# A routed expert layer: gate weights applied before the rows are stored, and gathers that add into the residual

## The chip, the cores and the metric

The kernel runs on one core of a Trainium2 chip. The time is that of the device for one launch, in microseconds (us). The core has a matrix engine (PE, its weight loads shown apart as PEld), a vector engine (DVE), an activation engine (ACT), a general engine (GpSimd, shown as POOL) and SyncE (SP), which here only starts transfers. DVE and ACT read PSUM, where PE writes; transfers and GpSimd reach only the on-chip memory (SBUF) and DRAM.

## What is computed

A decoder of two layers on x of shape 8 x 512 x 256, in float32, each layer with an attention, a cross attention and a feed-forward part, every part added to the residual stream. The change touches the first layer's feed-forward part, a mixture of 32 experts of which each token takes 4, and the part right after it, a linear recurrence. Cut to what matters:

```python
def L0_ffn(x):                                # xf: 4096 tokens x 256
    scores = softmax(xf @ Wg)                 # 32 gates for each token
    weights, indices = top_k(scores, 4)
    for e in range(32):
        pos = nonzero(pair_expert == e, size=C, fill_value=P)
        out = (silu(xg @ W1[e]) * (xg @ W3[e])) @ W2[e] * w[:, None]
        y = y.at[tok].add(out)
    return y + swiglu(xf, Ws1, Ws2, Ws3)      # and a shared expert
x = x + L0_ffn(layernorm(x))
def L1_attn(u):                               # h = h * A + u_t over the 512 positions
    return hs @ BC
x = x + L1_attn(layernorm(x))
```

## The kernel before

x stays in SBUF as `x[P, NT, D]`: 32 tiles of 128 tokens by 256 numbers, four tiles (`TB`) to a batch, eight batches (`B`). Each engine runs a program of its own, in the order in which it is written, and waits on semaphores. Stages end with a barrier. Three stages follow one another in `mix_experts_routed` and `mix_recurrence`.

**Ahead of them** the gates of all tokens are computed (`gates`, `[P, 32 tiles, 32 experts]`), and for each token and each of its four choices the row in which it shall stand (`place`): the rows of DRAM tensor `places` are sorted by expert, each expert filled up to whole tiles of 128, 160 tiles in all (`TILES`). `places` was cleared during the first attention by 23 transfers on SP (L2441).

**The scatter stage** (L1651 to L1777). For each batch and tile DVE writes the normalized rows `xn` and the indices `now` (L1738, L1740). GpSimd waits for them and issues four indirect transfers (L1694, `TOP` = 4), which scatter the tile's 128 rows of 1 KB to `places`. Buffer j is written again when its four scatters have landed (`scattered[j]`). DVE then works out from `rank`, `top` and `gates` the four weights of each token (`weight`, L1744 to L1750) and serves the shared expert, which PE and ACT compute. After batch 0 it also builds the table that says which expert each of the 160 tiles has (L1766 to L1771; `expert_h` and `expert_y`, the same table at two offsets).

**The expert stage** (L1782 to L1917). 160 tiles, in loops of `UNROLL` = 8. SP loads a tile of `places` to `xt` (L1805, eight buffers) as soon as PE has transposed the tile that stood there (`xp_full`), and stores the result `y` to DRAM tensor `outputs` (L1809) four tiles later. PE transposes, multiplies by `w1`, transposes, multiplies by `w2`, each a tile or more behind the other, and loads the expert numbers of eight tiles to registers at each turn. DVE forms `hid` (L1905) and copies the product out of PSUM to `y` (L1911).

**The gather stage** (`mix_recurrence`). For each batch, tile and choice GpSimd issues an indirect transfer (L639) that gathers 128 rows of `outputs` into a buffer `row`. DVE waits for a pair of tiles, adds weight times row into x (L698, eight multiply-adds for a pair, those of one tile in turn), gives GpSimd the next indices (`now`, L703), and goes on with the recurrence: of this batch the statistics and `xn`, of the batch before the scan (L735), of the one before that the addition of the result (L728). PE transposes and multiplies, ACT takes a square root.

An adding scatter stands already in the last stage of the kernel, the second layer's experts: L2287 adds 128 rows (`oa`) and 32 rows (`ob`) for each of 64 experts into `out` in DRAM, and L2277 gathers as many rows (`xa`, `xb`, 1280 bytes each).

## Time and profile before

| | us |
|---|---|
| median of 3 runs | 2944.31 |
| lowest, highest | 2944.04, 2954.93 |
| the profiled execution | 2948.37 |
| its span in the trace | 2946.6 |
| PE busy | 2320.9 (79%) |
| DVE busy | 1308.5 (44%) |
| ACT busy | 825.8 (28%) |
| GpSimd busy | 813.1 (28%) |

The profile is that of one execution. The span goes from the first to the last recorded instruction. A share of the whole span says little here, since the kernel is a row of stages with different limits, so the stages have to be looked at one by one. A row of a timeline has the start and the length in us, then engine, line, operation, the tile written and the tiles read; what stands in brackets is how long the engine had been idle and what ended that. Of an indirect transfer, the length is what GpSimd spends on issuing it; the data lands later, and "to landing" is counted from the start of the issue.

### The profile page before, as it was taken

The numbers are of one execution on the slowest core, as the hardware profiler recorded it, in microseconds if no ns is written. First come the engines' busy times: TensorE is split into PE (matmuls) and PEld (weight loads), VectorE is DVE, ScalarE is ACT, GpSimd is POOL, SyncE is SP. The second block draws the span as 40 slices with busy tenths as digits, with TensorE's granted clock in tenths as the row PEclk, the third lists the DMA queues.
The fourth block names the chain that finished last, engine by engine and source line by source line (L and its number), as shares of the span: only waits on it lengthen the run. The fifth ranks groups of instructions, "written<-read, shape, count | busy, mean of one in ns | idle before, by whom it ended". The sixth has DMA issues, their size and how long they took to land. (4 is left out here: it accounts for less than half of the span.)

```text
span 2946.6 us, 41569 instructions
## 1 busy us (share of the span) xinstructions
PE 2320.9 (79%) x12030; PEld 1614.8 (55%) x12031; DVE 1308.5 (44%) x2759; ACT 825.8 (28%) x1860; POOL 813.1 (28%) x1110
## 2 busy tenths in 40 slices
PE   5888656355799913348888888589988999999998
PEld 2444643133677712223333333245548999999997
DVE  4344225543233337747676665474442222222222
ACT  1111211111344410026666666122211222121221
POOL 1000000167100057412112120022224544455543
PEclk9999766677899966669999999789999999999999
DMA  8200110252444423232222220220005777777775
GB/s 268 94 0 0 47 40 1 84 204 102 138 146 146 143 87 100 62 101 91 84 84 82 82 67 1 81 100 15 14 21 182 239 254 237 245 251 237 253 242 168
DMA packets 191238, 353.01 MB, mean 120 GB/s; under 512 B 29302, under 2 KB 165983, under 8 KB 182984
## 3 DMA queue, kind: packets, MB, share of 16 engines
q1 hardware_dynamic: 160456, 294.68, 29.2%
q0 software_dynamic: 30720, 57.60, 8.1%
q8 instruction: 27, 0.44, 0.1%
q14 instruction: 35, 0.29, 0.0%
HBM read 259.21 MB, written 92.40 MB: 119 GB/s over the span
## 5 line engine op out<-in xcount | busy, mean ns | idle before, releaser
L2342 PE MATMUL me_hp<-me_xgT,me_w 128*128 128x160 f32 x3072 | 440.4, 300 | 0.8 <-DVE me_xgT L2384 0.6
L2342 PEld LDWEIGHTS me_hp<-me_xgT,me_w 128*128 128x128 f32 x3072 | 424.6, 191 | 1.9 <-DVE me_xgT L2384 0.7
L1335 DVE TENSOR_REDUCE hd_nmax<-hd_wide 128x2 f32<-128x1024 f32 x256 | 306.5, 1220 | 151.2 <-PE hd_wide L1127 151.1
L1286 ACT ACTIVATE hd_prob<-hd_slim 128x512 f32<-128x512 f32 x512 | 275.8, 601 | 158.7 <-PE hd_slim L1138 158.0
L2398 DVE TENSOR_TENSOR me_hid<-me_act_out,me_hp 128x160 f32<-128x160 f32 x384 | 123.2, 321 | 372.1 <-ACT me_act_out L2370 372.1
L2351 PE MATMUL me_op<-me_hid,me_w 128*128 128x160 f32 x1536 | 235.9, 303 | 0.0
L1127 PE MATMUL hd_wide<-hd_k_stack,hd_q_stack 97*128 97x512 bf16 x512 | 198.8, 393 | 34.9 <-DVE hd_rest L1330 15.0
L639 POOL DMA_INDIRECT rc_row<-outputs,rc_now x128 | 129.5, 1011 | 345.4 <-DVE rc_now L685 306.4
L2370 ACT ACTIVATE me_act_out<-me_hp 128x160 f32<-128x160 f32 x384 | 116.4, 303 | 358.1 <-PE me_hp L2342 358.1
L2351 PEld LDWEIGHTS me_op<-me_hid,me_w 128*128 128x128 f32 x1536 | 213.7, 190 | 2.6
L1138 PE MATMUL hd_slim<-hd_q_stack,hd_k_stack 100*128 100x512 bf16 x512 | 195.1, 384 | 16.5 <-DMA hd_q_stack<-hd_nrows 11.1
L2055 PE MATMUL me_r_hp<-me_r_xnT,me_r_sw 128*128 (+1 forms) x384 | 168.9, 600 | 10.9 <-DMA me_r_sw<-in_L_ffn_shared_w2T 10.9
L1852 PE MATMUL mr_e_hp<-mr_w,mr_e_xtT 128*128 x640 | 167.3, 384 | 0.8 <-issue 0.6
L1150 PE MATMUL hd_pv<-hd_prob,hd_v 128*32 128x512 f32 x1024 | 136.4, 604 | 6.6 <-ACT hd_oT L1252 6.2
L1138 PEld LDWEIGHTS hd_slim<-hd_q_stack,hd_k_stack 100*128 100x128 bf16 x512 | 49.5, 98 | 167.2 <-ACT hd_prob L1286 71.2
L1694 POOL DMA_INDIRECT places<-mr_s_xn,mr_s_now x128 | 125.8, 983 | 52.4 <-issue 36.0
L652 PE MATMUL rc_outp<-rc_wbc,rc_hid 128*128 128x256 f32 x128 | 46.8, 544 | 108.8 <-DVE rc_hid L735 108.8
L1905 DVE TENSOR_TENSOR mr_e_hid<-mr_e_act_out,mr_e_hp 128x128 f32<-128x128 f32 x160 | 46.1, 288 | 192.3 <-ACT mr_e_act_out L1884 192.3
L2055 PEld LDWEIGHTS me_r_hp<-me_r_xnT,me_r_sw 128*128 128x128 f32 x384 | 73.9, 193 | 101.1 <-issue 89.7
L2044 POOL TENSOR_TENSOR me_r_hid<-me_r_act_out,me_r_up_out 128x512 f32<-128x512 f32 x48 | 65.2, 1358 | 214.8 <-ACT me_r_up_out L2092 214.8
L2287 POOL DMA_INDIRECT out_x<-me_oa,me_then_a x64 | 104.4, 1631 | 68.7 <-issue 62.2
L1852 PEld LDWEIGHTS mr_e_hp<-mr_w,mr_e_xtT 128*128 128x128 f32 x640 | 110.1, 192 | 10.4 <-issue 1.6
(393 smaller groups left out, 3693.6 us busy)
## 6 DMA issues: line engine op xcount, KB each, us to landing
me_w<-in_L_ffn_w_exp SPq DMA_DIRECT2D x64, 2304.0 KB, 9.1
places<-z_zero SPq DMA_DIRECT2D x23, 896.0 KB, 10.1
mr_e_xt<-places SPq DMA_DIRECT2D x160, 128.0 KB, 2.0
outputs<-mr_e_y SPq DMA_DIRECT2D x160, 128.0 KB, 1.9
part_rows<-hd_parts SPq DMA_DIRECT2D x48, 256.0 KB, 2.3
hd_k_stack<-part_rows SPq DMA_DIRECT2D x192, 64.0 KB, 2.2
hd_q_stack<-part_rows SPq DMA_DIRECT2D x192, 64.0 KB, 2.2
mr_w<-in_L_ffn_w_in SPq DMA_DIRECT2D x4, 2048.0 KB, 18.2
```

Source lines behind the costliest of these rows:

```text
L639: nc.gpsimd.indirect_dma_start(out=row[:, j, n, :], out_offset=None, in_=outputs[:, :], in_offset=bass.IndirectOffsetOnAxis(ap=now[:, j, n ...
L1127: last = nc.tensor.matmul(wide[:, at, j, :], q_stack[0:FIRST_ROWS, bt.slot, h, qc * P:(qc + 1) * P], k_stack[0:FIRST_ROWS, bt.slot, h, :], ...
L1138: nc.tensor.matmul(slim[:, slim_slot(bt, item), :], k_stack[:, bt.slot, h, kc * P:(kc + 1) * P], q_stack[:, bt.slot, h, :], start=True, st ...
L1150: last = nc.tensor.matmul(pv[32 * j:32 * j + 32, :], v[:, slot, kc, head(g, j), :], prob[:, kc * GH + j, :], start=(kc == 0), stop=(kc == ...
L1286: nc.scalar.activation(prob[:, u, :], slim[:, slim_slot(bt, item), :], ACT.Exp, scale=D ** -0.5)\
L1335: nc.vector.tensor_reduce(nmax[:, g % 2, n // 2, c:c + 2], wide[:, at], AX.X, ALU.max, negate=True)\
L1694: nc.gpsimd.indirect_dma_start(out=places[:, :], out_offset=bass.IndirectOffsetOnAxis(ap=now[:, j, n:n + 1], axis=0), in_=xn[:, j, :], in_ ...
L1852: last = nc.tensor.matmul(hp[:, v, 0:2 * F], xtT[:, v, c, :], w1[:, bass.ds(e, 1), c, :].rearrange("p a n -> p (a n)"), start=(c == 0), st ...
L2055: last = nc.tensor.matmul(hp[:, f % 2, half, :], sw1[:, c, at:at + P], xnT[:, c, bass.ds(b * S, S)], start=(c == 0), stop=(c == DC - 1))
L2342: last = nc.tensor.matmul(hp[:, f % 3, half * CAP:(half + 1) * CAP], w1[:, sl, c, cols], xgT[:, sl, c, :], start=(c == 0), stop=(c == DC - 1))
L2351: last = nc.tensor.matmul(op[:, c, 0:CAP], w2[:, sl, f, c * P:(c + 1) * P], hid[:, sl, f, :], start=(f == 0), stop=(f == FC - 1))
L2398: nc.vector.tensor_tensor(hid[:, sl, f, :], act_out[:, f % 2, :], hp[:, f % 3, 0:CAP], ALU.mult).then_inc(h_free, 1)
```

## The change

Each scattered row carries the 32 gates of its token behind its 256 numbers, so rows of `places`, `xn` and `xt` have 288 numbers and the scattered ones come with a small copy on DVE. In the expert stage the copy of the product out of PSUM becomes a multiplication by one column of `xt`, the gate of the tile's expert, whose number DVE reads from a register; DVE loads eight such registers at each turn of the loop. Since `xt` is now read until then, SP loads a slot only behind the store of the tile that stood there. The match that gave `weight` goes. In the gather stage the buffer `row` and the multiply-adds go: each gather adds into x by itself (`compute_op=ALU.add`). Two additions into a tile may not overlap, so GpSimd waits before each for the one before it in the same tile, and takes the four tiles in turn for each choice. Its loop over the batches is written out.

```diff
@@ mix_recurrence, GpSimd
-                with pool.Fori(0, B) as b:
-                    for j in range(TB):
-                        pool.wait_ge(now_ready, b * TB + j + 1)
-                        pool.sem_inc(passed, 1)
-                        for n in range(TOP):
-                            nc.gpsimd.indirect_dma_start(out=row[:, j, n, :], out_offset=None, in_=outputs[:, :],
-                                                         in_offset=bass.IndirectOffsetOnAxis(ap=now[:, j, n:n + 1], axis=0))\
-                                .then_inc(gathered[j], 16)
+                for b in range(B):
+                    for n in range(TOP):
+                        for j in range(TB):
+                            if n == 0:
+                                pool.wait_ge(now_ready, b * TB + j + 1)
+                            else:
+                                pool.wait_ge(gathered[j], (b * TOP + n) * 16)
+                            pool.sem_inc(passed, 1)
+                            nc.gpsimd.indirect_dma_start(out=x[:, b * TB + j, :], out_offset=None,
+                                                         in_=outputs[:, :],
+                                                         in_offset=bass.IndirectOffsetOnAxis(ap=now[:, j, n:n + 1], axis=0),
+                                                         compute_op=ALU.add).then_inc(gathered[j], 16)
@@ mix_recurrence, DVE
-                    for pair in range(0, TB, 2):
-                        for j in range(pair, pair + 2):
-                            dve.wait_ge(gathered[j], b * 16 * TOP + 16 * TOP)
-                        for m in range(2 * TOP):
...
-                            nc.vector.scalar_tensor_tensor(xs, row[:, j, n, :], weight[:, bass.ds(t, 1), n], xs, ALU.mult, ALU.add)\
-                                .then_inc(taken, 1)
-                        dve.wait_ge(taken, (b * TB + pair + 2) * TOP)
+                    for j in range(TB):
+                        dve.wait_ge(gathered[j], (b + 1) * 16 * TOP)
                         if more:
-                            for j in range(pair, pair + 2):
-                                nc.vector.tensor_copy(now[:, j, :], place[:, b * TB + j + TB, :]).then_inc(now_ready, 1)
+                            nc.vector.tensor_copy(now[:, j, :], place[:, b * TB + j + TB, :]).then_inc(now_ready, 1)
@@ mix_experts_routed, the scatter stage
-                            nc.vector.tensor_scalar(xn[:, j, :], x[:, t, :], mean[:, bass.ds(t, 1)], rstd[:, bass.ds(t, 1)],
+                            nc.vector.tensor_scalar(xn[:, j, 0:D], x[:, t, :], mean[:, bass.ds(t, 1)], rstd[:, bass.ds(t, 1)],
                                                     ALU.subtract, ALU.mult).then_inc(rows_ready, 1)
+                            nc.vector.tensor_copy(xn[:, j, D:D + E], gates[:, t, :]).then_inc(rows_ready, 1)
                             nc.vector.tensor_copy(now[:, j, :], place[:, t, :]).then_inc(rows_ready, 1)
...
-                        nc.vector.tensor_tensor(match[:], rank[:, ts, :].unsqueeze(2).to_broadcast(wide),
-                                                top[:, ts, 0:TOP].unsqueeze(3).to_broadcast(wide), ALU.is_equal).then_inc(matched, 1)
-                        dve.wait_ge(matched, b * 2 + 1)
-                        nc.vector.tensor_tensor(match[:], match[:], gates[:, ts, :].unsqueeze(2).to_broadcast(wide), ALU.mult)\
-                            .then_inc(matched, 1)
-                        dve.wait_ge(matched, b * 2 + 2)
-                        nc.vector.tensor_reduce(weight[:, ts, :], match[:], AX.X, ALU.add).then_inc(weighed, 1)
@@ mix_experts_routed, the expert stage
-                            if not last:
-                                sp.wait_ge(xp_full, n + 1)
-                                load(n + UNROLL, u)
                             if not (first and u < LAG_S):
                                 store(n - LAG_S, (u - LAG_S) % UNROLL)
+                                if not (last and u >= LAG_S):
+                                    load(n - LAG_S + UNROLL, (u - LAG_S) % UNROLL)
...
+                        dve.load(regs_y, expert_y[0:1, bass.ds(i * UNROLL, UNROLL)])
...
-                                nc.vector.tensor_copy(y[:, v, :], yp[:, v % 2, 0:D]).then_inc(y_ready, 1)
+                                e = dve.snap(regs_y[u], min_val=0, max_val=E - 1)
+                                nc.vector.tensor_scalar(y[:, v, :], yp[:, v % 2, 0:D], xt[:, v, bass.ds(e + D, 1)], None, ALU.mult)\
+                                    .then_inc(y_ready, 1)
@@ program
-        ("places", [161 * P, D], F32), ("outputs", [161 * P, D], F32),
+        ("places", [161 * P, D + 32], F32), ("outputs", [161 * P, D], F32),
-            zero = Kit(nc, early, "z_").sb("zero", [P, ROWS, D])
+            zero = Kit(nc, early, "z_").sb("zero", [P, ROWS, D + 32])
```

GpSimd, the gather stage, before: the head of the loop and its first tile. `rc_now` holds the indices, `rc_row` the gathered rows.

```order
L634 UNCONDITIONAL_BRANCH
L634 ISA
L639 DMA rc_row<-outputs,rc_now 128x256 [waits rc_now_ready]
L639 DMA rc_row<-outputs,rc_now 128x256 x3
L636 REGISTER_ALU
```

GpSimd, the same place in the changed kernel: batch 0 as far as its second addition into each tile. `all_x` is the residual stream.

```order
L641 DMA all_x<-outputs,rc_now 128x256 [waits rc_now_ready] x4
L641 DMA all_x<-outputs,rc_now 128x256 [waits all_gathered0]
L641 DMA all_x<-outputs,rc_now 128x256 [waits all_gathered1]
L641 DMA all_x<-outputs,rc_now 128x256 [waits all_gathered2]
L641 DMA all_x<-outputs,rc_now 128x256 [waits all_gathered3]
```

Four gathers of one tile in a row have become one of each of the four tiles, and from the second round on each waits for the landing of the one before it in its tile.

DVE in the expert stage, before: the first tile of its loop.

```order
L1914 ISA
L1905 TENSOR_TENSOR mr_e_hid<-mr_e_act_out,mr_e_hp 128x128 [waits mr_silu_done]
L1908 REGISTER_ALU
L1910 REGISTER_ALU [waits mr_yp_full]
L1911 COPY mr_e_y<-mr_e_yp 128x256 [waits mr_y_stored5]
L1904 REGISTER_ALU
```

DVE, the same place in the changed kernel.

```order
L1900 ISA
L1883 TENSOR_LOAD mr_expert_y
L1889 TENSOR_TENSOR mr_e_hid<-mr_e_act_out,mr_e_hp 128x128 [waits mr_silu_done]
L1892 REGISTER_ALU
L1894 REGISTER_ALU [waits mr_yp_full]
L1895 ISA [waits mr_y_stored5]
L1896 TENSOR_SCALAR mr_e_y<-mr_e_yp,mr_e_xt 128x256
```

A load of registers stands at the loop's head, ahead of the first `hid`, and the copy has become a multiplication by a column of `xt` with one instruction more ahead of it.

SP in the expert stage, before: one tile of its loop.

```order
L1805 ISA [waits mr_xp_full]
L1805 DMA mr_e_xt<-places 128x256
L1808 REGISTER_ALU
L1809 ISA [waits mr_y_ready]
L1809 DMA outputs<-mr_e_y 128x256
```

SP, the same place in the changed kernel: the wait for PE's transpose is gone, and the load stands behind the store.

```order
L1791 ISA [waits mr_y_ready]
L1791 DMA outputs<-mr_e_y 128x256
L1787 ISA
L1787 DMA mr_e_xt<-places 128x288
L1790 REGISTER_ALU
```

The store has moved ahead, and the load is issued after `y` of the tile four before is done.

## Rows read from the trace of the kernel before

**Rows 1.** Stretches: length, busy of PE, PEld, DVE, ACT, POOL, clock, DMA share, GB/s.
```profile
570.00:753.00 183.00, 102.74 (x256) 60.06 (x256) 63.49 (x131) 19.82 (x24) 126.05 (x129) 0.75 0.46 165
753.00:1049.00 296.00, 268.79 (x1440) 220.24 (x1440) 107.58 (x320) 132.56 (x480) 0.00 (x0) 0.98 0.45 142
1049.00:1253.00 204.00, 55.03 (x192) 43.89 (x192) 131.14 (x355) 11.91 (x16) 129.46 (x128) 0.63 0.29 84
```

**Rows 2.** Timeline of the gather stage: start, length, engine, operation, [idle before <-releaser].
```profile
1055.25 1.01 POOL L639 DMA_INDIRECT rc_row<-outputs,rc_now  x1 [306.42 <-DVE rc_now L685]
...
1222.76 0.95 POOL L639 DMA_INDIRECT rc_row<-outputs,rc_now  x1 [0.30 <-issue]
1225.61 3.26 DVE L698 SCALAR_TENSOR_TENSOR all_x<-rc_row,rt_weight,all_x 128x256 f32<-128x256 f32 x8 [5.24 <-DMA rc_row<-outputs,rc_now]
1228.90 1.28 DVE L728 TENSOR_TENSOR all_x<-all_x,rc_outp 128x512 f32<-128x512 f32 x2
...
1251.26 1.41 DVE L731 BATCH_NORM_STATS2 all_stats<-all_x 128x6 f32<-128x256 f32 x4
```

**Rows 3.** Tile `rc_row`: min/median/max in ns, first and last start, landing.
```profile
L639 POOL DMA_INDIRECT rc_row<-outputs,rc_now x128: 949/953/2066, 1055.2 to 1222.8; - x128
...
DMA to landing us min/median/max: 2.7/2.7/3.8
```

**Rows 4.** Line 1694, the scatters: the same columns.
```profile
L1694 POOL DMA_INDIRECT places<-mr_s_xn,mr_s_now x128: 965/969/1810, 572.1 to 747.9; - x128
```

**Rows 5.** Timeline of the scatter stage, batch 1 and the last scatter.
```profile
604.78 0.15 DVE L1740 COPY mr_s_now<-rt_place 128x4 int32<-128x4 int32 x1
...
605.74 1.81 POOL L1694 DMA_INDIRECT places<-mr_s_xn,mr_s_now  x1 [12.57 <-DVE mr_s_now L1740]
...
606.74 0.69 DVE L1747 TENSOR_TENSOR mr_s_match<-mr_s_match,mr_gates 128x512 f32<-128x512 f32 x1
...
747.87 0.96 POOL L1694 DMA_INDIRECT places<-mr_s_xn,mr_s_now  x1 [0.30 <-issue]
```

**Rows 6.** Timeline of the expert stage, around a turn of its loop.
```profile
768.49 0.42 DVE L1911 COPY mr_e_y<-mr_e_yp 128x256 f32<-128x256 f32 x1
769.26 0.43 PE L1846 MATMUL mr_e_xp<-all_ident,mr_e_xt 128*128 128x128 f32 x2 [0.81 <-issue]
...
770.96 0.29 DVE L1905 TENSOR_TENSOR mr_e_hid<-mr_e_act_out,mr_e_hp 128x128 f32<-128x128 f32 x1 [2.05 <-ACT mr_e_act_out L1884]
...
783.57 0.43 PE L1846 MATMUL mr_e_xp<-all_ident,mr_e_xt 128*128 128x128 f32 x2 [1.01 <-issue]
```

**Rows 7.** GpSimd in the last stage, by form: count | busy us, mean ns | idle before.
```profile
L2287 POOL DMA_INDIRECT out_x<-me_oa,me_then_a x62 | 101.2, 1632 | 66.9 <-issue 62.2 <-POOL me_then_b L2269 4.7
L2287 POOL DMA_INDIRECT out_x<-me_ob,me_then_b x61 | 82.9, 1360 | 18.6 <-issue 18.6
L2277 POOL DMA_INDIRECT me_xa<-token_rows,me_now_a x59 | 62.0, 1051 | 53.2 <-POOL me_now_b L2269 51.0 <-issue 2.2
L2277 POOL DMA_INDIRECT me_xb<-token_rows,me_now_b x59 | 52.3, 887 | 18.0 <-issue 18.0
```

**Rows 8.** DMA queue of GpSimd: packets, MB, share; 1055 to 1223, 2236 to 2940 us.
```profile
q0 software_dynamic: 6048, 16.52, 34.0%
...
q0 software_dynamic: 16944, 22.67, 17.9%
```

**Rows 9.** GpSimd from 2217 to 2230 us, by form, ahead of the first scatter.
```profile
L2277 POOL DMA_INDIRECT me_xa<-token_rows,me_now_a x3 | 2.9, 981 | 2.5 <-POOL me_now_b L2269 2.5
```

**Rows 10.** Tile `me_oa`: ns min/median/max, and the landing of its scatters.
```profile
L2390 DVE TENSOR_SCALAR me_oa<-me_tp,me_xa x64: 476/477/486, 2235.8 to 2935.1; 128x256 f32<-128x256 f32 x64
...
DMA to landing us min/median/max: 3.8/4.5/4.6
```

**Rows 11.** The page, DMA issues: count, KB each, us to landing.
```profile
places<-z_zero SPq DMA_DIRECT2D x23, 896.0 KB, 10.1
mr_e_xt<-places SPq DMA_DIRECT2D x160, 128.0 KB, 2.0
```

More of the change, by code:

```diff
@@ L581, in mix_correlation, with mix_recurrence @@
         s.clear()
-def mix_recurrence(nc, ctx, x, ident, stats, mean, rstd, outputs, gathered, place, weight, decay_in, w_bc):
+def mix_recurrence(nc, ctx, x, ident, stats, mean, rstd, outputs, gathered, place, decay_in, w_bc):
     with ExitStack() as own:
@@ L592, in mix_recurrence @@
         TOP = place.shape[2]
-        row = k.sb("row", [P, TB, TOP, D])
         now = k.sb("now", [P, TB, TOP], I32)
@@ L1511, in softmax_scores, with mix_experts_routed @@
     chain.link(nc.vector.tensor_tensor(logits[:], logits[:], total[:].unsqueeze(2).to_broadcast([P, NT, n]), ALU.mult))
-def mix_experts_routed(nc, ctx, x, ident, mean, rstd, w_gate, w_in, w_out, places, outputs, scattered, place, weight):
+def mix_experts_routed(nc, ctx, x, ident, mean, rstd, w_gate, w_in, w_out, places, outputs, scattered, place):
     with ExitStack() as own:
@@ L1655, in mix_experts_routed @@
             k2 = Kit(nc, own2, "mr_s_")
-            xn = k2.sb("xn", [P, TB, D])
+            xn = k2.sb("xn", [P, TB, D + E])
             now = k2.sb("now", [P, TB, TOP], I32)
@@ L1671, in mix_experts_routed @@
             y_full, y_free = s.sem("sh_y_full"), s.sem("sh_y_free")
-            numbered, tabled, matched, weighed = s.sem("numbered"), s.sem("tabled"), s.sem("matched"), s.sem("weighed")
+            numbered, tabled = s.sem("numbered"), s.sem("tabled")
             with nc.Block() as block:
@@ L1690, in _ @@
                         for j in range(TB):
-                            pool.wait_ge(rows_ready, (b * TB + j) * 2 + 2)
+                            pool.wait_ge(rows_ready, (b * TB + j) * 3 + 3)
                             pool.sem_inc(passed, 1)
@@ L1754, in batch @@
                         dve.wait_ge(y_full, b + 1)
-                        dve.wait_ge(rows_ready, b * 2 * TB + 2 * TB)
+                        dve.wait_ge(rows_ready, b * 3 * TB + 3 * TB)
                         for m in range(2):
@@ L1783, in mix_experts_routed @@
             k2 = Kit(nc, own2, "mr_e_")
-            xt = k2.sb("xt", [P, UNROLL, D])
+            xt = k2.sb("xt", [P, UNROLL, D + E])
             xtT = k2.sb("xtT", [P, 2, DC, P])
@@ L1897, in _ @@
                     dve.sem_inc(y_ready, 2)
+                    regs_y = [dve.alloc_register(f"weigh_y{u}") for u in range(UNROLL)]
                     def steps(i, first, last_ones):
+                        dve.load(regs_y, expert_y[0:1, bass.ds(i * UNROLL, UNROLL)])
                         for u in range(UNROLL):
@@ L2442, in clear_rows @@
                         .then_inc(cleared, 16)
-                sp.dma_start(outputs[(n_tiles - 1) * P:n_tiles * P, :], zero[:, 0, :]).then_inc(cleared, 16)
+                sp.dma_start(outputs[(n_tiles - 1) * P:n_tiles * P, :], zero[:, 0, 0:D]).then_inc(cleared, 16)
             with nc.Block() as block:
@@ L2469, in program @@
             place = r.sb("place", [P, NT, TOP], I32)
-            weight = r.sb("weight", [P, NT, TOP])
             mix_experts_routed(nc, ctx, x, ident, mean, rstd, a["L0_ffn_Wg"], a["L0_ffn_w_in"], a["L0_ffn_w_out"], places, outputs,
-                               scattered, place, weight)
-            mix_recurrence(nc, ctx, x, ident, stats, mean, rstd, outputs, gathered, place, weight, a["L1_attn_A"], a["L1_attn_BC"])
+                               scattered, place)
+            mix_recurrence(nc, ctx, x, ident, stats, mean, rstd, outputs, gathered, place, a["L1_attn_A"], a["L1_attn_BC"])
         norm_stats(nc, ctx, "l1x", x, stats, mean, rstd, fresh=True)
```

11 lines of the change are left out of this document (1 added, 10 removed).

## The prediction

> **What bounds the kernel now.** I read first the table of busy times by stage [rows 1]. The change touches three stages that follow one another: the scatter stage (570 to 753 us), the expert stage (753 to 1049) and the gather stage, which also holds the recurrence (1049 to 1253). The reader is to see that PE, the busiest engine of the whole, is idle for most of the first and the last: 102.74 of 183 us and 55.03 of 204 us. It is busy 268.79 of 296 us in the middle one.
>
> Next I read the gather stage in order of time [rows 2]. GpSimd issues the first gather at 1055.25 and the last, the 128th, at 1222.76, which is 127 steps of 1.319 us. A gather occupies GpSimd for 0.953 us by the median [rows 3], and 0.30 us pass before the next. An undisturbed step is thus 1.258 us, 127 of them are 159.8 us, and the remaining 7.7 us are gathers that took longer. DVE stands waiting for the last pair of tiles: its multiply-add starts at 1225.61, 2.85 us after the last gather's issue. From 1228.90, when it ends, a serial tail of the last batches runs to 1252.67, and then the next stage begins. So this stage lasts as long as 128 issues on GpSimd, plus a landing, plus a tail. DVE's arithmetic between them is beside the path, but for the last eight multiply-adds (3.29 us).
>
> The scatter stage is bound by the same engine in the same way: a scatter takes 0.969 us by the median [rows 4], and from 605.74 to 747.87 there are 111 steps of 1.280 us [rows 5].
>
> The expert stage goes by PE. DVE, SP and their transfers have room: where PE turns around its loop it waits 0.81 us for nothing but its own registers and branch, and DVE then idles 2.05 us; eight tiles take 14.31 us [rows 6].
>
> **The gather stage, part by part.** Removed from DVE are 128 multiply-adds. All but the last eight lie beside GpSimd's issues, so their going gives nothing by itself. The last eight give 3.29 us. With them goes most of what stretched the gathers: the 7.7 us above. The scatter stage, in which DVE does less, has (1.280 - 1.273) x 111 = 0.8 us of such stretch, so I leave 1 us and book a gain of 6.7.
>
> Added is the addition inside each gather. No row shows a gather that adds. The nearest rows are the scatters of the last stage that add into `out` [rows 7]: 1.632 us for 128 rows and 1.360 us for 32 rows, against 1.051 and 0.887 us for that stage's plain gathers of as many rows. Adding costs GpSimd 0.58 us at 128 rows and still 0.47 us at 32. Direction is no explanation: the plain scatter and the plain gather of 128 rows differ by 0.016 us (0.969 and 0.953) [rows 3, 4]. The packets say that an adding DMA is built differently. The 126 or so plain gathers of the gather stage make 6048 packets, 48 each, for 128 rows. The last stage has some 62 experts with a plain gather of 128 rows (48) and of 32 rows (32), and 16944 packets, 273 for an expert; 193 are left for the two adding scatters with 160 rows together, so a row has a packet of its own [rows 8]. I take this as a price of the addition and not of its target.
>
> The last stage makes GpSimd a little slower than here: its own 128-row gathers take 0.981 us while no scatter is yet in it [rows 9] and 1.051 us later. The adding gather then lies between 0.953 + 0.58 = 1.53 us and 1.63 us. I take 1.55, near the lower end, since the plain gather of this stage is the one that it replaces. With the 0.30 us gap a step is 1.855 us, and 127 steps are 235.6 us where 159.8 stood: 75.8 us more. The ends of the price that I keep for the range are 1.36 us, what 32 adding rows take (127 x 0.19 = 24 us less), and 1.66 us plus a gap of 0.31 (15 us more).
>
> Added too is a wait for each gather: the next addition into a tile is not issued before the one before it has landed. Behind it on GpSimd are all the later gathers, and DVE waits for these. A tile's turn comes every fourth step, 7.4 us after its last issue. Plain gathers land after 2.7 us, at most 3.8 [rows 3]; adding scatters of 128 rows land after 4.5 us, at most 4.6, in a stage whose queues are fuller [rows 10]. So the wait is over 2.8 us before it is asked: nothing. At the batch's turn DVE copies `now` once a tile's last gather has landed, some 4.6 us after issue, and DVE has been waiting by then: it is busy 131 us in the whole stage before, multiply-adds among it, which is 16.4 us for a batch, and the new batch takes 16 x 1.855 = 29.7 us. Nothing again.
>
> The tail: the last landing comes about 4.0 us after its issue where it was 2.85, and the 3.29 us of multiply-adds are gone: -2.1.
>
> Gather stage: +75.8 - 6.7 - 2.1 = **+67.0 us**.
>
> **The scatter stage.** Rows become 1152 bytes instead of 1024. The 128-row gather of 1280 bytes takes 0.981 us [rows 9] against 0.953 for 1024; a quarter to a half of 0.028 us on 112 scatters is 1 us. The number of scatters stays. DVE loses three wide operations in a batch (0.69 us each) and gets four small copies (0.15 us each, as the `now` copies) [rows 5]. Before the first scatter of batch 1, for which GpSimd waits 12.57 us, DVE builds the table, and ahead of that it waits for PE; the operations lost in batch 0 lie before that wait and give nothing, and the scatter comes one small copy later: 0.2. From there DVE is ready before GpSimd, with more room than before. **+1 us**, bounds 0 and +4.
>
> **The expert stage.** The copy out of PSUM, 0.42 us, becomes a multiplication by a column of `xt`; the same form stands in the last stage with 0.477 us [rows 10]. 0.05 us more moves nobody where DVE's two operations, 0.42 and 0.29 us, share the 1.79 us of a tile. New is a load of eight registers on DVE at each turn of the loop. PE loads sixteen there and loses 0.81 us; DVE is free from 768.91 to 770.96, 2.05 us [rows 6]. Cover: 1.2 us. If it were gone, 20 turns would pay. On SP the load of a slot now stands behind the store, hence behind `y_ready`: it is issued about four tiles ahead (7 us) instead of seven and lands after 2.0 us [rows 11], so 5 us of cover stay. Behind it on SP is only the next store. **0 us.**
>
> **The clearing of `places`** gets an eighth more bytes (23 transfers of 896 KB [rows 11] become 1008 KB) on a queue that nobody waits for in the attention stage. 0 us, at most 1.
>
> **Sum:** +67.0 + 1 = **+68 us**. The profiled run took 2948.37 us (span 2946.6 and 1.8 around it), 4.1 above the median of the three. It would become 3016; from the median, 2944.3 + 68 = **3012 us**.
>
> **Rivals.** *A: the addition is done by the DMA engines and costs GpSimd nothing* (the side of no loss). Against it are both adding kinds of [rows 7]; for it, only that these write to DRAM and these gathers write to SBUF. Place: every step of the gather stage; price of 0.58 us gone. The stage then gives 6.7 + 2.1 back and the sum is -9 + 1 = -8: 2936 us. It comes out at no loss as soon as the adding gather costs less than about 0.07 us above the plain one, since 127 x 0.07 is the 9 us of gain. The Trainium skill, "DMA: Bandwidth & Descriptors", section "SWDGE vs HWDGE vs iDMA", says that GpSimd computes one pair of descriptors for each DMA operation, a read and a write, and names no extra for one that adds. By that rule this rival would be right; the trace disagrees for scatters, 1.632 against 1.051 us. Chance 0.10.
>
> *B: half price.* An addition into SBUF needs less preparation than one into DRAM: about 1.25 us each, 127 x 0.3 = 38 us less than forecast, 2974 us. No row speaks for it but the missing case. 0.07.
>
> *C: the landing takes over.* If a 128-row adding gather took longer than 7.4 us to land, GpSimd would wait for each. At 9 us a step is 2.25 us and the time is 3012 + 50 = 3062 us. Against it: 4.6 us at most [rows 10]. For it: one packet a row, and a read of two sources. 0.06.
>
> *D: DVE's register load is long*, 3 us rather than under 1. Then each of 20 turns loses about 1 us: 3032 us. Against it is PE's 0.81 us for twice as many registers. 0.05.
>
> **How the numbers follow.** The forecast has 0.72: its own range is 2986 (1.36 us each) to 3030. With B at the lower and D at the upper side the range of 8 in 10 is 2980 to 3042; outside lie A, B and C. A measurement of this kernel tells apart about 0.5%, 15 us. Faster by more than that needs under 2930 us, which no case gives: 0.03 for what I have not seen. Within 0.5%: A, 0.11. Slower: 0.86.
>
> **What would show it.** In the profile after: adding gathers on GpSimd of 1.5 to 1.65 us, 0.30 us apart, with no waits for a landing; the gather stage about 65 us longer; PE's turn in the expert stage unchanged at 14.3 us for eight tiles; scatters at 0.97 to 0.98 us. I am wrong if the adding gather takes about 0.95 us (A), if GpSimd's idle time names the DMA (C), or if PE's wait at the loop's turn grows (D).

## The result and the profile after

| | before | after |
|---|---|---|
| median, us | 2946.94 | 3014.63 |
| lowest, highest, us | 2944.04, 2954.93 | 3005.80, 3027.62 |
| the profiled execution, us | 2948.37 | 3006.31 |
| its span, us | 2946.6 | 3004.5 |

The changed kernel is slower: the ratio of the times is 1.0229, with a 95% interval of 1.0177 to 1.0280. The medians lie 67.7 us apart. On a second chip the same pair gave 3019.64 against 2957.00 us, a ratio of 1.0220 (1.0179 to 1.0261).

The first view is the one that the prediction began with, the table of busy times by stretch, now of the kernel after: length, busy time of PE, PEld, DVE, ACT and GpSimd (with the number of instructions), granted clock of PE, DMA share, GB/s. The three rows answer to those of [rows 1].

```profile
570.00:754.70 184.70, 105.20 (x256) 61.53 (x256) 53.25 (x140) 19.82 (x24) 124.67 (x129) 0.74 0.48 175
754.70:1050.00 295.30, 269.89 (x1440) 221.23 (x1440) 123.60 (x320) 132.74 (x480) 0.00 (x0) 0.98 0.50 151
1050.00:1321.50 271.50, 55.06 (x192) 43.80 (x192) 79.13 (x227) 11.91 (x16) 198.89 (x128) 0.60 0.45 63
```

Only the last row has grown by much. DVE has lost 52 us of work there and GpSimd has got 69.43 us more (198.89 against 129.46) for the same 128 instructions; the stretch itself is longer by about as much. The adding gathers themselves, by their source line, in the kernel after (name, count, ns min/median/max, first and last start, then the idle time before them by what ended it, then who waited):

```profile
L641 POOL DMA_INDIRECT all_x<-outputs,rc_now x128: 1542/1552/1665, 1056.3 to 1292.4; - x128
its engine sat idle before it (us, times) until:
  DVE rc_now L688: 305.7, 1
  issue: 36.9, 121
  DMA all_x<-outputs,rc_now: 1.8, 6
...
  DVE rc_now L695: 153.3, 28
...
DMA to landing us min/median/max: 3.7/3.8/3.9
```

Where [rows 3] had 953 ns for one gather and 2.7 us to its landing, there are now 1552 ns and 3.8 us. The largest is 1665 ns: nothing stretches them any more. Six gaps name a landing, with 1.8 us together, which is 0.30 us each and thus the gap that every gather has; GpSimd has waited for no landing. DVE, on the other hand, waits 153 us for gathers. In order of time the end of the stage reads so (columns as in [rows 2]):

```profile
1292.37 1.55 POOL L641 DMA_INDIRECT all_x<-outputs,rc_now  x1 [0.30 <-issue]
1296.38 1.29 DVE L720 TENSOR_TENSOR all_x<-all_x,rc_outp 128x512 f32<-128x512 f32 x2 [20.30 <-DMA all_x<-outputs,rc_now]
...
1319.27 1.41 DVE L723 BATCH_NORM_STATS2 all_stats<-all_x 128x6 f32<-128x256 f32 x4
```

From the issue of the last gather to the first addition of the recurrence's result there are 4.01 us; before there were 6.14 (1222.76 to 1228.90 in [rows 2]), 2.85 for the landing and 3.29 for eight multiply-adds.

To compare stages across kernels I cut each profiled run at the same five events: the first scatter, the last scatter, the first gather, the last gather, and the start of the next stage. All are in us.

| | before | after | after minus before | predicted |
|---|---|---|---|---|
| first scatter to last | 175.8 | 177.2 | +1.4 | +1 |
| last scatter to first gather | 307.4 | 306.7 | -0.7 | 0 |
| first gather to last | 167.5 | 236.0 | +68.5 | +69.1 |
| last gather to next stage | 34.7 | 33.6 | -1.1 | -2.1 |
| sum | 685.4 | 753.5 | +68.1 | +68 |

The two spans differ by 57.9 us only, and that is no contradiction. The way to the first scatter takes 572.1 and 572.4 us, but the part behind the three stages takes 1689.1 us before and 1678.5 after, with no instruction changed in it. 8.8 of these 10.6 us lie in one stretch of the second layer; here it is by the same columns as above, first in the kernel before, then in the one after:

```profile
1855.60:1978.60 123.00, 92.39 (x280) 49.08 (x281) 67.82 (x169) 24.80 (x32) 18.81 (x11) 0.82 0.25 85
```

```profile
1923.30:2037.50 114.20, 84.67 (x280) 45.82 (x281) 69.27 (x169) 24.80 (x32) 16.75 (x11) 0.89 0.27 91
```

The same 280 matmuls keep PE busy for 92.39 and 84.67 us, and the granted clock is 0.82 and 0.89. Such stretches differ from one run to the next, whatever the kernel: up to the first scatter, where all kernels of this study are alike but for the size of the clearing, the profiled runs took from 570.7 to 585.8 us. That is why the runs below are compared by the events first, and by the total only where enough runs stand behind it.

### The profile page after: what moved, and what is told of

It reads as the page before. It is cut to its first block and busy times, and to the rows that moved or that the text cites. A ratio compares the mean times of both kernels' runs of the same rounds, so it can differ in the third digit from the quotient of the medians.

```text
span 3004.5 us, 41474 instructions
## 1 busy us (share of the span) xinstructions
PE 2316.3 (77%) x12030; PEld 1614.0 (54%) x12031; DVE 1263.7 (42%) x2640; ACT 825.8 (27%) x1860; POOL 879.7 (29%) x1110
## 3 DMA queue, kind: packets, MB, share of 16 engines
q0 software_dynamic: 43008, 59.70, 10.1%
## 5 line engine op out<-in xcount | busy, mean ns | idle before, releaser
L641 POOL DMA_INDIRECT all_x<-outputs,rc_now x128 | 198.9, 1554 | 344.4 <-DVE rc_now L688 305.7
L2337 PE MATMUL me_op<-me_hid,me_w 128*128 128x160 f32 x1536 | 236.0, 304 | 0.0
L1119 PE MATMUL hd_wide<-hd_k_stack,hd_q_stack 97*128 97x512 bf16 x512 | 198.5, 393 | 35.1 <-DVE hd_rest L1322 15.0
L1685 POOL DMA_INDIRECT places<-mr_s_xn,mr_s_now x128 | 124.4, 972 | 55.3 <-issue 32.9
L655 PEld LDWEIGHTS rc_outp<-rc_wbc,rc_hid 128*128 128x128 f32 x128 | 35.8, 287 | 179.6 <-DVE rc_hid L727 171.7
```

Of the source, the lines that this page charges most:

```text
L641: nc.gpsimd.indirect_dma_start(out=x[:, b * TB + j, :], out_offset=None, in_=outputs[:, :], in_offset=bass.IndirectOffsetOnAxis(ap=now[:, ...
L1119: last = nc.tensor.matmul(wide[:, at, j, :], q_stack[0:FIRST_ROWS, bt.slot, h, qc * P:(qc + 1) * P], k_stack[0:FIRST_ROWS, bt.slot, h, :], ...
L1685: nc.gpsimd.indirect_dma_start(out=places[:, :], out_offset=bass.IndirectOffsetOnAxis(ap=now[:, j, n:n + 1], axis=0), in_=xn[:, j, :], in_ ...
L2337: last = nc.tensor.matmul(op[:, c, 0:CAP], w2[:, sl, f, c * P:(c + 1) * P], hid[:, sl, f, :], start=(f == 0), stop=(f == FC - 1))
```

## The experiments

My theory was that of the prediction: the whole loss is the price that GpSimd pays for issuing an indirect transfer that adds, and this price belongs to the instruction more than to its rows. The rivals were that the loss comes from elsewhere in the change (the wider rows, DVE's new operation in the expert stage, the order of the gathers, the written-out loop), that the wait for the landing costs part of it, and that the price goes by rows. The first four kernels ran on one chip, where the kernel before took 2959.44 us (2951.81 to 2967.71); the other three on another, where it took 2957.00 (2944.45 to 2964.27). The stretches between the events, in us, of all runs:

| | scatters | to first gather | gathers | behind | sum |
|---|---|---|---|---|---|
| before | 175.8 | 307.4 | 167.5 | 34.7 | 685.4 |
| after | 177.2 | 306.7 | 236.0 | 33.6 | 753.5 |
| after once more | 177.7 | 306.2 | 236.0 | 33.3 | 753.2 |
| plain gathers into x | 177.3 | 306.2 | 161.4 | 32.8 | 677.6 |
| DVE adds | 174.5 | 306.0 | 162.3 | 35.1 | 677.9 |
| DVE adds, once more | 176.6 | 306.6 | 163.8 | 34.6 | 681.6 |
| tile by tile | 178.2 | 306.6 | 500.0 | 32.4 | 1017.1 |
| 32 rows added | 177.3 | 306.7 | 211.1 | 33.2 | 728.3 |
| DVE adds, table early | 164.5 | 306.0 | 162.4 | 34.9 | 667.8 |

### The same kernel without the addition

```diff
-                                                         in_offset=bass.IndirectOffsetOnAxis(ap=now[:, j, n:n + 1], axis=0),
-                                                         compute_op=ALU.add).then_inc(gathered[j], 16)
+                                                         in_offset=bass.IndirectOffsetOnAxis(ap=now[:, j, n:n + 1], axis=0)).then_inc(gathered[j], 16)
```

The gathers overwrite the tile of x instead of adding to it, so the addition of the routed results is left out. All else of the change stands, its order and its waits too.

> The changed kernel, but its 128 gathers write plainly over the tiles of x instead of adding into them; waits, order and everything else stay. The addition, and with it the routed result and the residual up to there, is left out. Theory (the addition itself is what costs GpSimd): a gather takes 0.95 to 0.98 us instead of 1.552, the step is 1.26 us, the gather stage is 127 x 0.60 = 76 us shorter and the kernel takes 2930 to 2942 us, below the kernel before. Rival (the wait on each landing, the order or the written-out loop cost part of it): the step stays above 1.35 us or GpSimd's idle time names the DMA, and the time is 2950 us or more.

Measured: 2944.46 us (2934.62 to 2950.61), 0.9935 of the kernel before (0.9911 to 0.9959). The gathers by their line:

```profile
L641 POOL DMA_INDIRECT all_x<-outputs,rc_now x128: 949/953/1107, 1069.3 to 1230.6; - x128
...
  DVE rc_now L694: 2.0, 2
...
DMA to landing us min/median/max: 2.7/2.7/3.1
```

One argument of the instruction was taken away, and with it went 599 ns of each gather, 1.1 us of each landing, and 74.7 us of the time between first and last gather (236.03 to 161.36), where 127 x 0.599 is 76.1. The other 1.4 us are two gaps in which GpSimd now waits for indices from DVE, 2.0 us together where two plain gaps take 0.6. The rest of the change, left alone, is not slower than the kernel before. The forecast in microseconds looks missed by a little (2944 against at most 2942) only because the kernel before stood at 2959 on this chip; as a difference it is -15, where the events show -7.8 (677.6 against 685.4), the remainder being within what untouched stretches vary.

### The weighting alone: plain gathers, DVE adds

```diff
-                for b in range(B):
-                    for n in range(TOP):
-                        for j in range(TB):
...
-                            nc.gpsimd.indirect_dma_start(out=x[:, b * TB + j, :], out_offset=None,
...
+                            nc.gpsimd.indirect_dma_start(out=row[:, j, n, :], out_offset=None, in_=outputs[:, :],
...
-                        dve.wait_ge(gathered[j], (b + 1) * 16 * TOP)
+                            dve.wait_ge(gathered[j], b * 16 * TOP + 16 * TOP)
...
+                            nc.vector.tensor_tensor(xs, row[:, j, n, :], xs, ALU.add).then_inc(taken, 1)
```

The first half of the change stays (gates in the rows, weighting out of PSUM), the second is undone: the gather stage is that of the kernel before, with an addition where the multiply-add stood.

> The weighting part of the change alone: gates travel with the rows and are applied as the product leaves PSUM, but the gathers write plainly to the row buffer as before and DVE adds the rows (128 plain additions of two tiles). Theory: the weighting part costs nothing on the path, so the time is that of the kernel before within 3 us, 2942 to 2950 us; the gather stage is as long as before (204 us). The stretch of the gathers (7.7 us before, 0.5 us with the adding gathers) comes back if DVE's operations on two tiles in SBUF cause it. Rival: the loads behind the stores, the register loads or the wider rows cost something, 5 to 15 us more than before, in the expert or the scatter stage.

Measured: 2946.41 us (2933.93 to 2956.00) against 2959.44, 0.9953 (0.9930 to 0.9976). On the second chip the same kernel was run again, for a closer verdict:

> The kernel of e2_dve_adds once more, so that the next one can be held against it: weights applied in the expert stage, plain gathers, DVE's plain additions. Theory (it shortens the stretch of the gathers and the scatter stage by 7 to 8 us together): 0.994 to 0.998 of the kernel before. Rival (the 13 us of e2_dve_adds were a drift of the chip): a ratio whose interval holds 1.

Measured: 2950.33 us (2931.89 to 2955.57) against 2957.00, 0.9977 (0.9952 to 1.0001). The weighting half therefore costs nothing that can be measured and may bring a quarter to half a per cent. Both expectations come out only in part. The first had the time within 3 us of the kernel before, and it is 13 us below it on that chip, clear of 1 by its interval. The second named an interval that holds 1 as the sign that those 13 us were the chip's drift, and the interval does hold 1, by a hair; so a gain in the total is not shown. By the events the sum is 677.9 and 681.6 against 685.4 us. Where the few microseconds come from is in the gathers (first of the two runs):

```profile
L639 POOL DMA_INDIRECT rc_row<-outputs,rc_now x128: 949/953/1154, 1060.9 to 1223.2; - x128
```

Undisturbed, 127 steps would be 159.8 us. With the multiply-adds DVE had stretched them by 7.7 us, in the one profile that there is of that kernel; with plain additions, which read two tiles of SBUF just as well, it is 2.5 and 4.0 us, and 2.6 in the last kernel below. Of the 4.0 us, 1.7 belong to a single gather, which took 2.702 us:

```profile
L639 POOL DMA_INDIRECT rc_row<-outputs,rc_now x128: 947/953/2702, 1068.0 to 1231.8; - x128
```

This I had not thought: half of the stretch or more goes with the multiplication alone, without taking DVE out of the stage. Eight additions take 2.77 us in that trace where eight multiply-adds take 3.26 [rows 2], so they are a little shorter, but by 15% only; whether it is the form of the operation or its place beside the issues that counts, no run here tells apart.

### Four additions to one tile in a row

```diff
-                    for n in range(TOP):
-                        for j in range(TB):
+                    for j in range(TB):
+                        for n in range(TOP):
```

Only the order of the adding gathers is changed; now three of four wait for the landing of the one just before.

> The changed kernel with the two inner loops of GpSimd swapped: the four additions into one tile follow one another, each after the landing of the one before. Theory: the wait, free in the changed kernel since a tile's turn comes every 7.4 us, is now paid: three steps in four take the landing time, 3.8 us and a little more, 32 x (3 x 4.0 + 1.86) = 443 us where 236 stood, and the kernel takes about 3220 us. Rival (what is waited for is done when the issue ends, and only the issue counts): 3005 to 3030 us as the changed kernel.

Measured: 3284.65 us, one run. By the gathers' line, then in order of time:

```profile
L641 POOL DMA_INDIRECT all_x<-outputs,rc_now x128: 1541/1550/1631, 1069.3 to 1569.3; - x128
...
  DMA all_x<-outputs,rc_now: 289.2, 95
...
DMA to landing us min/median/max: 3.6/3.8/3.9
```

```profile
1073.99 1.56 POOL L641 DMA_INDIRECT all_x<-outputs,rc_now  x1 [3.08 <-DMA all_x<-outputs,rc_now]
1078.57 1.54 POOL L641 DMA_INDIRECT all_x<-outputs,rc_now  x1 [3.02 <-DMA all_x<-outputs,rc_now]
```

Here the wait that the changed kernel has is laid open. A waited step takes 4.58 us (1073.99 to 1078.57): 3.8 to the landing, and 0.8 more before the next gather's row begins. I had taken the landing alone, 4.0, and so expected 443 us for the stage; 96 waited steps of 4.6 and 31 others of 1.85 make 499, and 500.0 were measured. That is most of what the forecast of 3220 us for the kernel fell short by. For the changed kernel this says how near the wait is: a tile's turn comes after four steps, 7.4 us, and 4.6 are needed. With two tiles in turn (3.7 us) it would wait; that was not run.

### Only 32 of 128 rows added

```diff
-                            nc.gpsimd.indirect_dma_start(out=x[:, b * TB + j, :], out_offset=None,
+                            nc.gpsimd.indirect_dma_start(out=x[0:32, b * TB + j, :], out_offset=None,
...
-                                                         in_offset=bass.IndirectOffsetOnAxis(ap=now[:, j, n:n + 1], axis=0),
+                                                         in_offset=bass.IndirectOffsetOnAxis(ap=now[0:32, j, n:n + 1], axis=0),
```

The other 96 rows of each tile are left without their routed results.

> The changed kernel, but each adding gather takes the first 32 of its 128 rows only; the other 96 rows of each tile stay without their routed result. Theory (the addition has a price for each instruction, 0.45 us or more, beside one for each row): an adding gather of 32 rows takes 1.27 to 1.36 us, the kernel 2978 to 2992 us. Rival (the price goes by rows alone, 0.60 us for 128 of them): 1.02 us, and the kernel takes about 2947 us.

Measured: 2997.42 us, one run. That is 38 us above the kernel before on this chip (2959.44); the forecast of 2978 to 2992 us, made from a kernel before of 2947, meant 31 to 45 us more.

```profile
L641 POOL DMA_INDIRECT all_x<-outputs,rc_now x128: 1343/1348/1502, 1068.6 to 1279.7; - x128
```

With a quarter of the rows a gather still takes 1.348 us. From 32 to 128 rows it grows by 0.204 us, 2.1 ns for a row. Carried on straight to no rows at all that leaves 1.28 us, an estimate from two points. The rival by which the price goes by rows wanted about 1.02 us and falls. The last stage had said the same of scatters, 1.360 us for 32 rows and 1.632 for 128 [rows 7], and its price for 32 rows is nearly the one measured here. A plain gather of 32 rows was not run in this stage. Since a plain one of 128 rows takes 0.953 us, and the last stage has the plain one cheaper at 32 rows than at 128, the addition costs 0.40 us or more at 32 rows; by the last stage it is 0.47 there and 0.58 at 128 rows. Splitting these gathers would not bring the time down: four of 32 rows need 4 x 1.65 us with their gaps, one of 128 needs 1.86.

### The changed kernel once more

> The changed kernel unaltered, beside the kernel before and the two below on one chip. Theory (the change costs 68 us between the first scatter and the stage behind the gathers, and the rest of its difference is PE's clock in stages that it does not touch): that stretch is again 753 to 754 us long against 685 before, while the time as a whole may scatter by some 10 us to either side of 68 us above the kernel before. Rival (the 58 us between the two profiled runs is the true price and something in the change gives 10 us back in later stages): the later stages are again 10 us shorter than those of the kernel before.

Measured: 3019.64 us (3017.05 to 3024.21) against 2957.00, that is 62.6 us more. The gathers take 236.0 us again, and the sum of the events is 753.2 where the first run had 753.5. The rival wanted the stages behind to be 10 us shorter again. They take 1685.3 us, where the first profile of this kernel had 1678.5 and that of the kernel before 1689.1; the other kernels, unchanged there, have 1681.3 to 1688.4. So those 10 us are no part of the change. Against the kernel with the weighting alone (681.6, same chip) the second half of the change costs 71.6 us, and against the medians of the same chip 69.3.

### The weighting alone, with the table built earlier

The profile before had shown GpSimd idle for 12.57 us in the scatter stage, until DVE wrote the rows of batch 1 [rows 5], since DVE first served the shared expert of batch 0 and built the expert table. This kernel starts from the one with plain gathers. DVE builds the table right behind the rows of batch 0 and writes the rows of the next batch ahead of the addition of this one's shared expert.

```diff
-                    def batch(b, sl, first):
+                    def rows(b, first):
...
+                    def batch(b, sl, more=True):
...
+                        if more:
+                            rows(b + 1, False)
...
-                    batch(0, 0, True)
+                    rows(0, True)
...
-                    batch(1, 1, False)
+                    batch(0, 0)
+                    batch(1, 1)
```

> The kernel of e6_dve_adds_again with one more edit in the scatter stage: DVE builds the table of experts right behind the rows of batch 0, and writes the rows of batch b + 1 ahead of the addition of batch b's shared result. Theory (GpSimd is the bound of this stage and stands idle 11 to 15 us for the first rows of batch 1): that idle time falls under 3 us, the scatter stage and the kernel get 10 to 14 us shorter than e6_dve_adds_again, about 0.990 of the kernel before. Rival (what is late next is the shared expert's chain through PE, which then ends the stage): GpSimd waits for DVE in later batches or the stage ends by PE, and nothing is gained.

Measured: 2931.46 us (2925.07 to 2939.66), 0.9926 of the kernel before (0.9904 to 0.9948): faster than either kernel of this case, by 25.5 us and by 88. The scatters by their line, first in the repeated run without this edit, then with it:

```profile
L1692 POOL DMA_INDIRECT places<-mr_s_xn,mr_s_now x128: 965/969/1342, 584.8 to 761.4; - x128
...
  DVE mr_s_xn L1736: 14.8, 1
```

```profile
L1692 POOL DMA_INDIRECT places<-mr_s_xn,mr_s_now x128: 965/969/1717, 570.7 to 735.3; - x128
its engine sat idle before it (us, times) until:
  issue: 32.9, 108
  DVE mr_s_now L1739: 7.0, 19
```

The one long idle time is gone, and the scatters take 164.5 us instead of 176.6. Of the 18.9 us between the two medians of this chip, 12.1 are this, within the 10 to 14 that were forecast; the rest lies in stretches that the edit does not touch, the gathers among them (1.4 us). The experiment confirms how the prediction read the scatter stage: what GpSimd waits for counts whole there. What DVE computes beside it is not free altogether: the scatters that now run beside the table's construction take longer (the last section shows them), and GpSimd's 128 scatters together take 126.8 us where they took 124.4. 14.8 us of idle time less these 2.4 are about the 12 that were won.

## Why the prediction was right

**What bounds the stage.** GpSimd's issues in a row. The run without the addition changed their length alone, and the stage followed by 74.7 of 76.1 us; the other 1.4 are a wait for indices that shorter gathers lay open.

**The price of an adding gather**, 1.55 us, was the term on which all hung, and no row showed such a gather. It measured 1.552. Two choices made it: to read the adding scatters of another stage as the price of the addition and not of the scatter or of its target, and to stay near the lower end, because the plain gathers of that stage are slower than here. 127 x (1.552 - 0.953) is 76.1 us where 75.8 had been summed. That it came so close is in part luck: the rows gave 1.53 to 1.63 us, which is 13 us over 127 steps, and nothing in them told 1.55 from the rest. The lower bound that I kept, 1.36 us, is what 32 rows cost, and has turned out to be just that, 1.348, and not a possible price for 128.

**The stretch** of the plain gathers was booked as 6.7 us of gain and 1 us left. With the gap at 0.305 us (36.9 us in 121 gaps), as it is in the 1.258 and 1.855 of the prediction, 127 undisturbed steps of 1.857 are 235.8 us, and 236.0 were measured: 0.2 us are left, so the gain was 7.5. The mechanism is right. What it belongs to is told more exactly by the experiments: a kernel that keeps DVE's additions and drops the multiplication gets 3.7 to 5.2 of these microseconds as well.

**The landing and the wait.** Forecast as about 4.0 us, measured 3.8 by the line and 4.01 at the end of the stage; the wait was free as said. The margin was put at 2.8 us (7.4 less 4.6 for the slowest landing of another stage). It is 2.8 us by chance, since it has other parts: 3.8 to land and, as the run tile by tile shows, 0.8 until GpSimd goes on.

**The tail** was to be 2.1 us shorter. It is, as far as the addition of the recurrence's result (6.14 to 4.01 us), but the whole way to the next stage is shorter by 1.1 only. Half of the other microsecond lies between that addition and the last statistics (22.36 us before, from 1228.90 to 1251.26; 22.89 after, from 1296.38 to 1319.27), and half between these and the next stage's first instruction (6.24 and 6.72 us). What lengthened them is open.

**The scatter stage** got +1.4 us for +1, and scatters of 1152 bytes take 0.969 us as those of 1024 did, by the median. So the wider row, for which the microsecond was booked, costs nothing, and that the number came out is luck. The idle time before batch 1, which I had put at 0.2 more, has grown from 12.57 to 15.34 us, and GpSimd's scatters together take 1.4 us less (124.67 us busy against 126.05 in [rows 1]); the two make 1.4. In the kernel before, then in the one after:

```profile
575.43 8.84 PE L1710 MATMUL mr_s_hp<-mr_xnT,mr_s_sw 128*128 x16 [18.97 <-DMA mr_s_sw<-in_L_ffn_w_out]
590.71 1.61 DVE L1766 TENSOR_TENSOR mr_s_past<-mr_s_tile_no,mr_ends 1x1408 f32<-1x1408 f32 x1
591.42 1.75 POOL L1694 DMA_INDIRECT places<-mr_s_xn,mr_s_now  x1 [0.30 <-issue]
```

```profile
576.62 10.05 PE L1701 MATMUL mr_s_hp<-mr_xnT,mr_s_sw 128*128 x16 [19.91 <-DMA mr_s_sw<-in_L_ffn_w_out]
593.12 1.61 DVE L1749 TENSOR_TENSOR mr_s_past<-mr_s_tile_no,mr_ends 1x1408 f32<-1x1408 f32 x1
608.24 1.01 POOL L1685 DMA_INDIRECT places<-mr_s_xn,mr_s_now  x1 [15.34 <-DVE mr_s_xn L1729]
```

PE's product for the shared expert of batch 0, for whose weights it waits, began later and took longer (8.84 and 10.05 us). So DVE began the table 20.7 us after the first scatter instead of 18.6, and 2.1 of the 2.8 us are this. The rest is that the last scatter of batch 0 took 1.75 us beside the table's first comparison in the kernel before, while in the one after it took 0.97 and was over before the table began, so GpSimd's idle time starts sooner. This is no cost of the change that could be told from chance: the two runs of the kernel with DVE's additions, alike to the letter but run on two chips, have 11.4 and 14.8 us of this idle time, and 174.5 and 176.6 us from first scatter to last.

**The expert stage** was put at nothing and moved by -0.7 us. The turn of the loop in the kernel after:

```profile
771.95 0.43 PE L1827 MATMUL mr_e_xp<-all_ident,mr_e_xt 128*128 128x128 f32 x2 [0.77 <-issue]
...
773.65 0.29 DVE L1889 TENSOR_TENSOR mr_e_hid<-mr_e_act_out,mr_e_hp 128x128 f32<-128x128 f32 x1 [1.82 <-ACT mr_e_act_out L1865]
...
786.13 0.43 PE L1827 MATMUL mr_e_xp<-all_ident,mr_e_xt 128*128 128x128 f32 x2 [0.90 <-issue]
...
L1883 DVEq TENSOR_LOAD <-mr_expert_y x21: 594/600/850, 754.8 to 1040.9; - x21
```

PE's own pause is 0.77 and 0.90 us where it was 0.81 and 1.01 [rows 6]; DVE still idles 1.82 us at the turn, and its register load, 0.60 us by the median of the last line (of the view by tile), is over at 772.17, 1.48 us before the turn's first `hid`. It delays nothing: that `hid` starts 1.70 us after PE's transposes in both kernels ([rows 6] has 769.26 to 770.96 before, 771.95 to 773.65 after). The multiplication out of PSUM costs DVE more than the 0.05 us a tile that were counted: it is busy 123.60 us in this stage where it was 107.58, 0.10 us a tile, and nobody waits for it. Eight tiles take 14.18 us. The loads of `xt`, now behind the stores, and the clearing of `places` are seen on the page after (KB each, us to landing):

```profile
places<-z_zero SPq DMA_DIRECT2D x23, 1008.0 KB, 11.0
mr_e_xt<-places SPq DMA_DIRECT2D x160, 144.0 KB, 2.2
```

They land after 2.2 us instead of 2.0, and after 11.0 instead of 10.1 [rows 11], and nobody waits for either.

**The rivals.** That the DMA engines do the addition at no cost to GpSimd fell with the first trace, and the pair of runs with and without it puts the difference at 0.599 us. The Trainium skill, "DMA: Bandwidth & Descriptors", section "SWDGE vs HWDGE vs iDMA", has one pair of descriptors for each DMA operation and names no extra for one that adds; here the one that adds takes 0.599 us more and makes more packets, and the measurement decides. Here is GpSimd's queue during the gathers (packets, MB, share of the engines): in the kernel after from 1056 to 1293 us, with plain gathers into x from 1069 to 1232, and with 32 rows added from 1068.5 to 1282:

```profile
q0 software_dynamic: 18171, 16.55, 50.4%
...
q0 software_dynamic: 6096, 16.65, 35.1%
...
q0 software_dynamic: 6128, 4.20, 15.0%
```

For some 126 gathers the first is 144 each, where [rows 8] gave 48; the bytes are the same. Plain gathers into x make 48 again, so it is the addition and not the tile written. The additions of 32 rows make 48 as well and yet take 1.348 us where a plain gather with as many packets takes 0.953: the price does not follow the number of packets. Half price, a landing that takes over, and a long register load are excluded by the rows above.

**The total.** 68 us had been summed, 67.7 lie between the medians, 68.1 between the events. The mechanism is borne out, and the last microsecond is luck: the interval of the ratio spans 52 to 82 us, the second chip gave 62.6, and terms that were each off by up to a microsecond (the stretch, the tail, the expert stage) cancel. Two small slips are in the prediction's numbers. Its low end of 2986 us should be 2987 or 2988 (3012 - 24, less the scatter stage's 1), and its chances for the slower side add up to 0.90 where it says 0.86, since those of the forecast and the four rivals make 1.00 and leave no room for the 0.03 of the unseen.

## What to carry to other kernels

An indirect transfer that adds is not a plain one with the arithmetic thrown in: the engine that issues it paid 0.6 us more for each at 128 rows, and most of its 1.55 us stays when the rows fall to 32 (1.35), so in a stage bound by that engine's issues the addition belongs on an engine that idles. When a change puts an operation in a place where no row shows it, look for its nearest relative in another stage, and correct it by how the plain form differs between the two stages. And when two profiled runs differ by less than the sum of your terms, cut both at the same events before you look for a missing term: here 10.6 us of it were in stretches that no edit touched.

## What the runs showed of the hardware

**GpSimd held up behind one form of DVE's work.** With the table built early, scatters run beside its construction. In order of time, in that kernel:

```profile
574.36 1.61 DVE L1759 TENSOR_TENSOR mr_s_past<-mr_s_tile_no,mr_ends 1x1408 f32<-1x1408 f32 x1
575.12 1.71 POOL L1692 DMA_INDIRECT places<-mr_s_xn,mr_s_now  x1 [0.30 <-issue]
...
576.01 1.61 DVE L1761 TENSOR_REDUCE mr_s_table<-mr_s_past 1x44 f32<-1x1408 f32 x1
...
577.13 0.97 POOL L1692 DMA_INDIRECT places<-mr_s_xn,mr_s_now  x1 [0.30 <-issue]
...
577.65 1.61 DVE L1759 TENSOR_TENSOR mr_s_past<-mr_s_tile_no,mr_ends 1x1408 f32<-1x1408 f32 x1
...
578.40 1.71 POOL L1692 DMA_INDIRECT places<-mr_s_xn,mr_s_now  x1 [0.30 <-issue]
```

A scatter that begins 0.76 us into the comparison of two tiles takes 1.71 us instead of 0.97, and ends 0.86 us after the comparison does (576.83 and 575.97; the second pair has 580.11 and 579.26). Beside the reduction, which reads one tile and lasts as long, it takes 0.97. The kernel before has such a scatter too, 1.75 us beside its first comparison. The operation touches a single partition. The Trainium skill, "SBUF — State Buffer", section "Summary: rules for kernel authors", says that where DVE has two SBUF inputs while the GpSimd operation reads SBUF, the second one to issue is blocked until the first has finished; these rows agree, with 1.71 us against 0.97. The Trainium skill, "SBUF — State Buffer", section "Who interferes with whom", reports a probe in which `tensor_tensor` did not stall a transfer of GpSimd's; here it did, by 0.74 us, and the measurement decides. What the rows leave open is why 128x256 additions of two SBUF tiles stretch the gathers by 2.5 to 4.0 us in all while the multiply-adds of the same tiles did by 7.7.

**The pause behind a landing.** GpSimd goes on 0.8 us after the landing that it waits for (steps of 4.58 us for landings of 3.8). A chain of transfers that wait for one another pays this each time.

**The landing too gets longer by the addition**, 3.8 against 2.7 us at 128 rows. Counted from the end of the issue that is 2.2 against 1.7 us, so 0.6 of the 1.1 us are the longer issue itself. In the kernel with 32 rows the landing comes after 2.9 us.
